# Gate logits from transposed fp16 parts of the rows instead of from rows turned on TensorE

## The chip, the core and the metric

The kernel is one program on one NeuronCore of a Trainium2 chip. The metric is the device time in microseconds. The engines are TensorE (PE, with its weight loads as PEld), VectorE (DVE), ScalarE (ACT), GpSimd (POOL) and the queue engine SyncE (SP), which here only issues transfers. ACT and POOL issue some transfers as well.

## The reference

Input x is 8 x 512 tokens of 256 numbers. First attention, then a mixture of experts, both on normalised rows and both added to what they got:

```python
x = x + attn(layernorm(x), W_qkv, b_qkv, W_out, b_out)   # 16 heads of 16, causal
xn = layernorm(x) * gamma + beta
probs = softmax(xn @ gate_w)                             # 8 experts
w, idx = top_k(probs, 2); w = w / sum(w)
h = gelu(xn @ w1[e] + b1[e]); out_e = h @ w2[e] + b2[e]  # 256 -> 1024 -> 256
x = x + sum over the two chosen e of w[e] * out_e
```

The kernel computes an expert only for the tokens that chose it.

## The kernel before, in words

**Stages.** From 0 to some 122 us the eight batches are normalised and projected to q, k and v. Then come 32 attention units of four heads each, four units to a batch. Behind them stand 39 expert tiles of up to 256 gathered tokens. Between these, the side work of each batch b runs: output projection, residual, second normalisation, the gate, the choice of two experts, the ranks in the experts' lists.

**Order.** Every engine goes through one timetable, written by hand: `at(tick, stage, n)`. A unit has 48 ticks, an expert tile 42; each engine takes its own stages in order of ticks, and waits for semaphores in them. So a wait in a stage holds up everything behind it on that engine. The side work of batch b is placed from a base 192 ticks after that of batch b - 1 (a batch is four units).

**A unit.** `combo` (L660) runs score matmuls on PE (L656 transposed, L628 and L641 for the maxima); ACT takes the exponential (L905, L902), DVE the maxima (L1225 to L1231); `weigh` (L700) multiplies with v. The transposed scores go round three PSUM banks (`TURNS`, banks 4, 5, 6). Side work takes its banks out of the same round (`take_side`), so the next use of a bank waits until the copy named in `TAKEN_BY` has emptied it. `keep_o`, `move_o`, `keep_inverse`, `move_inverse`, `load_unit`, `load_v` and `top_in` are transfers of a unit, issued by SP; `top_in` brings row maxima to the stack that the next unit's scores read.

**The side work that the change touches,** for batch b:

- `out_proj` (L714, L715) projects two halves of the tokens into a bank each; ACT's `copy_out` (L950) moves a half to `turned`; DVE's `add_out` (L1248) adds x, loaded again into `rows`, and writes `x2`.
- After normalisation `rows` holds xn scaled by a power of two; `acc_out` (L1974) stores the residual out of `x2`; then `row_high` on ACT (L940) and `row_low` on DVE (L1491, its instruction at L1067) write two fp16 parts of `rows` into the memory of `x2`, and `rows_out` (L1966) stores them.
- `turn_x` (L722): PE transposes `rows` in fp32, two groups of four 128x128 blocks; ACT's `copy_x` (L922) moves each group to `turned`.
- `gate` (L731): PE multiplies `turned` by `gate_w` in fp32 into a bank; `copy_gate` (L956) copies the 4 x 8 logits of a partition out; DVE's `choose` follows. `count` (L741) multiplies the choices by triangles of ones in bf16.
- `turned` is shared: `copy_out` of the next batch waits for the gate of the batch before.

**Expert stage.** POOL gathers 256 rows (L1703), SP turns them with transposing transfers (`turn_tokens`, L1887, 71 in all, each one chunk of 128 tokens by 512 fp16), PE does 48 matmuls (L775) and 48 (L793) a tile, ACT the gelu (L986), DVE splits it in two parts, POOL scatters (L1727).

Of the kernel before, what the change touches and what calls it, by code (L numbers as in the profile page):

```python
# [14 lines left out]
P = 128  # L15
# [46 lines left out]
def build(nc, t):  # L62
# [54 lines left out]
    with ctx:  # L117
# [17 lines left out]
        tops_dram = dram("tops_of_rows", (P, 5), F32)  # L135
# [8 lines left out]
        keep = Area(arena, 0, 3088 + 2 * TT - D // 2)  # L144
# [10 lines left out]
        gate_w = keep.take(KC * E, k=KC, e=E)  # L155
        minus_half = keep.take(2 * TT, n=2, t=TT)
# [20 lines left out]
        S_TOP, S_SCALE, S_TMP, S_UNDO = stat[:, 0:8], stat[:, 8:12], stat[:, 16:24], stat[:, 24:28]  # L177
        UNDO_1, UNDO_2 = stat[:, 28:29], stat[:, 29:30]
        SCALE_W = [S_SCALE[:, 0:1], S_SCALE[:, 1:2]]
        SCALE_X, SCALE_H = S_SCALE[:, 2:3], S_SCALE[:, 3:4]  # L180
# [23 lines left out]
        turned = a2.take(KC * T, k=KC, t=T)  # L204
# [10 lines left out]
        all_rows_tops = w_raw[1][:, 0:5 * P]  # L215
# [8 lines left out]
        one_more = a2.take(TT)  # L224
        logit = a2.take(TT * E, t=TT, e=E)
# [151 lines left out]
        for b in range(B):  # L377
# [60 lines left out]
        for j in range(-1, TILES):  # L438
# [10 lines left out]
            if j >= 0:  # L449
# [3 lines left out]
                if j + 2 < TILES:  # L453
# [9 lines left out]
        TAKEN_BY = {"top_turn": "top_copy", "out_proj": "copy_out", "turn_x": "copy_x", "gate": "copy_gate",  # L463
                    "count": "copy_count"}
# [99 lines left out]
        def tensor(pe):  # L564
# [153 lines left out]
            def turn_x(b, k):  # L718
                w.wait_ge(sem("beta_added"), b + 1)
                bank = take_side("turn_x", (b, k))  # L720
                for tt in range(TT):
                    m = pe.transpose(bank[:, tt * P:(tt + 1) * P], rows[:, tt, k * P:(k + 1) * P], ident)  # L722
                m.then_inc(sem("side_made"), 1)
# [84 lines left out]
            for stage, n in timetable:  # L808
# [8 lines left out]
                elif stage == "turn_x":  # L817
                    turn_x(*n)
                elif stage == "gate":
                    gate(n)  # L820
                elif stage == "count":
                    count(n)
                elif stage == "hidden":
                    hidden(*n)
                elif stage == "expert_out":
                    expert_out(*n)


        def scalar(act):
# [89 lines left out]
            def copy_x(b, k):  # L919
                w.wait_ge(sem("out_added"), KC * b + k + 1)  # L920
                w.wait_ge(sem("side_made"), side_made("turn_x", (b, k)))
                act.copy(turned[:, k, :], side_bank("turn_x", (b, k))).then_inc(sem("act_freed"), 1)  # L922

# [22 lines left out]
            def copy_out(b, half):  # L946
                w.wait_ge(sem("side_made"), side_made("out_proj", (b, half)))
                if b > 0:
                    w.wait_ge(sem("side_made"), side_made("gate", b - 1))
                act.copy(turned[:, half, :], side_bank("out_proj", (b, half))).then_inc(sem("act_freed"), 1)  # L950

            def copy_gate(b):
                w.wait_ge(sem("side_made"), side_made("gate", b))
                if b > 0:
                    w.wait_ge(sem("chosen"), b)
                act.copy(logit, side_bank("gate", b)[:, 0:TT * E].rearrange("p (t e) -> p t e", t=TT)).then_inc(  # L956
                    sem("act_freed"), 1)
# [56 lines left out]
            for stage, n in timetable:  # L1014
# [12 lines left out]
                elif stage == "copy_x":  # L1027
                    copy_x(*n)
# [32 lines left out]
        def vector(v):  # L1061
# [115 lines left out]
            def find_scales():  # L1177
# [5 lines left out]
                v.tensor_reduce(S_TMP[:, 4:5], b1_sb, AX.XY, ALU.max, apply_absolute_value=True).then_inc(sem("own_tops"), 1)  # L1183

            def find_scales_2():
                w.wait_ge(sem("all_tops"), 16)
                root = math.ceil(math.sqrt(D))
                m = own.mark(v.tensor_reduce(S_TOP[:, 0:5], all_rows_tops.rearrange("p (q c) -> p c q", c=5), AX.X,
# [8 lines left out]
                m = own.mark(both(S_TOP[:, 3:4], S_TOP[:, 3:4], S_TOP[:, 4:5], ALU.add))  # L1197
                w.wait_ge(own.sem, m)
                m = own.mark(v.tensor_scalar(S_TMP[:, 0:4].bitcast(I32), S_TOP[:, 0:4].bitcast(I32), 23, None,
                                             ALU.logical_shift_right))  # L1200
                w.wait_ge(own.sem, m)
                m = own.mark(v.tensor_scalar(S_TMP[:, 0:4].bitcast(I32), S_TMP[:, 0:4].bitcast(I32), 80.0, 200.0,
                                             ALU.max, ALU.min))
                w.wait_ge(own.sem, m)
                own.mark(v.tensor_scalar(S_TMP[:, 4:8].bitcast(I32), S_TMP[:, 0:4].bitcast(I32), -1.0,
                                         float(127 * 2 + 14), ALU.mult, ALU.add))
# [800 lines left out]
```

## Time and profile before

| | us |
|---|---|
| median of 3 runs | 970.67 (967.7 to 975.95) |
| the profiled execution, its own time | 969.97 |
| its span in the trace | 968.1 |
| PE busy, share of the span | 845.3, 87% |
| DVE busy | 703.9, 73% |
| ACT busy | 573.0, 59% |
| POOL busy | 470.0, 49% |
| mean granted TensorE clock | 0.926 of full |

Busy times are of one profiled execution. PE and PEld overlap. A wait is idle time of an engine just before an instruction, with the instruction or transfer whose end released it. SP's rows are issues of transfers: the time given is that of issuing, and the data land later. A batch's side work appears eight times, with b from 0 to 7: for b = 0 to 4 inside the attention units, for b = 5 at their end, for b = 6 and 7 in the expert stage.

### The profile page before, as it was taken

Reading aid. Unit: us, or ns where it says so; the run is one execution under the profiler, and the core shown is the slowest. Engines: PE = TensorE matmul, PEld = TensorE weight load, DVE = VectorE, ACT = ScalarE, POOL = GpSimd, SP = SyncE. Lnnn points to the kernel's source line nnn. Section 1 sums busy time; section 2 is a strip of 40 time slices with the busy share of each in tenths; the row PEclk is TensorE's granted clock in tenths of the full one; section 3 lists DMA queues with packets and bytes.
Section 4 is the critical chain, followed back from the end, with each engine's and each line's share of the span. In section 5 each row is a group of like instructions: output and inputs, shape, how many; then the busy total and the mean of one; then the engine's idle time right before and its main releaser. Section 6 shows DMA issues by size and latency. Waiting matters only on the chain.

```text
span 968.1 us, 21008 instructions
## 1 busy us (share of the span) xinstructions
PE 845.3 (87%) x6760; PEld 555.1 (57%) x6760; DVE 703.9 (73%) x1566; ACT 573.0 (59%) x1048; POOL 470.0 (49%) x575
## 2 busy tenths in 40 slices
PE   4899977877888978797887897989989999999996
PEld 3555422332433424342423695869868888888875
DVE  6677888878689797979895585766756766656664
ACT  2777466657787686868686462545525445445453
POOL 4100032325545747666567556665467554554441
PEclk9999978887998888898987898989999999999998
DMA  9888658745867676566727873444534444444341
GB/s 203 263 271 280 222 164 232 208 111 176 221 198 223 166 194 172 168 195 177 193 69 242 150 136 64 61 83 96 80 51 78 79 79 73 76 76 83 50 74 23
DMA packets 185046, 139.39 MB, mean 144 GB/s; under 512 B 98064, under 2 KB 167568, under 8 KB 184816
## 3 DMA queue, kind: packets, MB, share of 16 engines
q1 hardware_dynamic: 153840, 95.25, 38.5%
q0 software_dynamic: 15776, 18.95, 12.2%
q10 hardware_dynamic: 15328, 23.86, 7.5%
q8 instruction: 61, 1.00, 0.4%
q14 instruction: 41, 0.34, 0.1%
HBM read 83.63 MB, written 44.80 MB: 133 GB/s over the span
## 4 chain that ended last, share of the span: by engine, by line
PE 57%; DVE 16%; DMA 11%; issue 6%; SPq 4%; ACT 4%; another core or an unknown queue 1%; POOLq 0%; ACTq 0%; POOL 0%; DVEq 0%
PE banks L775 18%; PE banks L793 18%; PE banks L597 5%; PE banks L700 3%; DMA arena<-arena 3%; DVE arena L1228 3%; PE banks L714 3%; PE banks L656 3%; DMA weighed_values<-arena 2%; PE banks L587 2%; DVE weights L1390 2%; PE banks L641 2%; DVE arena L1067 2%; PE banks L628 2%; DVE arena L1230 1%
## 5 line engine op out<-in xcount | busy, mean ns | idle before, releaser
L986 ACT ACTIVATE arena<-banks,arena 128x256 f32<-128x256 f32 (+1 forms) x312 | 152.4, 541 | 207.3 <-issue 101.9
L775 PE MATMUL banks<-arena,weights 128*128 128x256 f16 (+1 forms) x1872 | 211.3, 269 | 16.2 <-issue 9.2
L793 PE MATMUL banks<-weights,arena 128*128 x1704 | 198.0, 275 | 5.9 <-DVE arena L1520 3.2
L775 PEld LDWEIGHTS banks<-arena,weights 128*128 x1872 | 176.2, 99 | 45.5 <-issue 20.3
L1727 POOL DMA_INDIRECT out<-arena x71 | 115.7, 1629 | 158.9 <-DVE arena L1531 113.9
L793 PEld LDWEIGHTS banks<-weights,arena 128*128 128x128 f16 x1704 | 165.8, 99 | 31.8 <-issue 9.9
L656 PE MATMUL banks<-arena 64*128 64x128 f16 (+3 forms) x512 | 119.8, 332 | 36.3 <-DMA arena<-arena 13.0
L1518 DVE TENSOR_SCALAR arena<-arena 128x512 f16<-128x512 f32 (+1 forms) x156 | 76.0, 487 | 76.2 <-ACT arena L986 57.1
L628 PE MATMUL banks<-arena 62*128 62x384 f16 (+3 forms) x512 | 94.3, 326 | 32.4 <-DVE arena L1225 11.7
L1520 DVE SCALAR_TENSOR_TENSOR arena<-arena 128x512 f16<-128x512 f32 (+1 forms) x156 | 110.2, 706 | 5.5
L656 PEld LDWEIGHTS banks<-arena 64*128 64x128 f16 x512 | 38.1, 99 | 123.2 <-issue 39.7
L1228 DVE TENSOR_REDUCE arena<-banks 128x2 f32<-128x1024 f32 x64 | 77.9, 1217 | 30.0 <-PE banks L641 29.7
L905 ACT ACTIVATE arena<-banks,arena 128x512 f32<-128x512 f32 x128 | 81.4, 686 | 21.4 <-PE banks L656 20.9
L905 ACT ACTIVATE weights<-banks,arena 128x512 f32<-128x512 f32 x128 | 80.4, 683 | 15.9 <-PE banks L656 15.7
L1703 POOL DMA_INDIRECT arena<-token_rows,arena x71 | 77.3, 1089 | 21.1 <-issue 18.6
L1674 POOL DMA_INDIRECT slot_tokens<-arena x64 | 68.0, 1062 | 26.0 <-issue 16.5
L1688 POOL TENSOR_SCALAR_AFFINE_SELECT weights<-weights 128x512 f32<-128x512 f32 (+1 forms) x80 | 47.7, 613 | 65.5 <-ACT weights L905 57.5
L1230 DVE TENSOR_REDUCE arena<-banks 128x2 f32<-128x768 f32 x64 | 60.8, 950 | 24.1 <-PE banks L641 21.1
L1531 DVE SCALAR_TENSOR_TENSOR arena<-banks,arena 128x256 f32<-128x256 f32 x71 | 31.4, 480 | 60.4 <-PE banks L793 43.1
L1688 POOL TENSOR_SCALAR_AFFINE_SELECT arena<-arena 128x512 f32<-128x512 f32 (+1 forms) x80 | 48.0, 617 | 35.4 <-ACT arena L905 34.0
L641 PE MATMUL banks<-arena 128*128 128x256 bf16 (+1 forms) x320 | 60.7, 275 | 0.0
L700 PE MATMUL banks<-arena 128*32 128x256 f32 (+3 forms) x512 | 58.0, 533 | 2.7 <-ACT arena L917 2.5
(199 smaller groups left out, 1257.1 us busy)
## 6 DMA issues: line engine op xcount, KB each, us to landing
weights<-in_L_ffn_w ACTq DMA_DIRECT2D x16, 1024.0 KB, 7.6
arena<-in_L_ffn_w SPq DMA_DIRECT2D x32, 512.0 KB
qk_parts<-weights SPq DMA_DIRECT2D x64, 128.0 KB
arena<-qk_parts SPq DMA_DIRECT2D x128, 64.0 KB, 3.3
weighed_values<-arena SPq DMA_DIRECT2D x32, 256.0 KB
token_rows<-arena SPq DMA_DIRECT2D x12, 512.0 KB, 4.3
arena<-qk_parts SPq DMA_DIRECT2D x128, 32.0 KB, 3.4
arena<-weighed_values SPq DMA_DIRECT2D x32, 128.0 KB
```

The lines of the kernel that those rows point to most:

```text
L628: pe.matmul(bank[:, to:to + (qt + 1) * P], q_st[u % 4][half, h, qt * P:qt * P + P], k_st[u % 4][half, h, 0:(qt + 1) * P], start=(to == 0), ...
L641: m = pe.matmul(masked, ident_h, mask, start=False, stop=True, skip_group_check=True)
L656: m = pe.matmul(turn_bank(number)[:, to:to + T - kt * P], k_st[u % 4][half, h, kt * P:kt * P + P], q_st[u % 4][half, h, kt * P:T], start=T ...
L700: m = pe.matmul(banks[32 * h:32 * h + 32, O_BANK, kt * P:T], v_and_ones(u, kt, h), p_T[u % 2][:, h, a:a + width], start=(kt == W_ORDER[0]) ...
L775: m = pe.matmul(bank[:, c * TILE:c * TILE + WIDTH[j]], w1[:, k, wp, f:f + P], xp[:, k, 0:WIDTH[j]], start=(i == 0), stop=(i == len(terms) ...
L793: m = pe.matmul(bank[:, c * D:(c + 1) * D], hp[:, f, c * P:(c + 1) * P], w2[:, f // (FC // 2), wp, f % (FC // 2), :], start=(f == 0 and i ...
L905: act.activation(p_T[u % 2][:, PAIR * h + j, PT_AT[kt]:PT_AT[kt] + T], bank, ACT.Exp, scale=EXP_SCALE).then_inc(sem("exped"), 1)
L986: m = act.activation(h_32[r % 2][:, c, 0:WIDTH[j]], banks[:, 1 + c2, c * TILE:c * TILE + WIDTH[j]], ACT.Gelu, bias=b1_now[j % 2][:, 2 * c2 ...
L1228: m = v.tensor_reduce(out[:, :, slot // 2, 3], pair, AX.X, ALU.max, negate=True)
L1520: v.scalar_tensor_tensor(h_low[:, pair, width], h_32[r % 2][:, :, width], SCALE_H, h_high[:, pair, width], ALU.mult, ALU.subtract).then_in ...
L1688: m = g.affine_select(out=area, in_=area, compare_op=ALU.is_ge, fill=0.0, base=0, pattern=pattern, channel_multiplier=-1)
L1727: g.indirect_dma_start(acc_dram[:, :], bass.IndirectOffsetOnAxis(slot_of(j, c), 0), y[j % 2][:, c, :], None, compute_op=ALU.add).then_inc( ...
```

## The change

The gate no longer reads rows turned by PE. `turn_x` and `copy_x` go. SP issues four transposing transfers a batch, `turn_rows`, each for 128 tokens, out of the fp16 parts in `x2` into a new buffer `rows_T` (in the memory of `turned`). The gate weights are split once into two fp16 parts (`gate_parts`), and the gate is 16 fp16 matmuls of 16 columns a batch in place of 8 fp32 ones: the high and low parts of the rows, each times both parts of the weights. `copy_gate` scales back; `choose` first adds the two halves of the logits. `copy_out` writes `x2` in place of `turned`, and `add_out` adds in place. Since the transfers read `x2`, `copy_out` of batch b + 1 waits for `rows_out` and `rows_turned` of batch b.

In the timetable `acc_out`, `row_high`, `row_low` and `rows_out` stand 10 ticks earlier, `gate` and `copy_gate` 28 ticks later; the choices stay where they were for b < 6 and come 24 ticks later for b = 6 and 7. The scales get one more number, for the gate weights.

```diff
-            at(base + 308, "acc_out", b)
-            at(base + 336, "row_high", b)
-            at(base + 344, "row_low", b)
-            at(base + 348, "rows_out", b)
-            for k in range(KC):
-                at(base + 331 + 14 * k, "turn_x", (b, k))
-                at(base + 336 + 14 * k, "copy_x", (b, k))
-            at(base + 372, "gate", b)
-            at(base + 377, "copy_gate", b)
-
-            base += 48 if b < B - 2 else 0
+            at(base + 298, "acc_out", b)
+            at(base + 326, "row_high", b)
+            at(base + 334, "row_low", b)
+            at(base + 338, "rows_out", b)
+            for tt in range(TT):
+                at(base + 342 + 6 * tt, "turn_rows", (b, tt))
+            at(base + 400, "gate", b)
+            at(base + 405, "copy_gate", b)
+
+            base += 48 if b < B - 2 else 24
...
             def gate(b):
-                w.wait_ge(*side_out("turn_x", (b, 1)))
-                w.wait_ge(sem("x_scaled"), 1)
+
+                w.wait_ge(sem("rows_turned"), 16 * TT * (b + 1))
+                w.wait_ge(sem("scales"), 1)
                 bank = take_side("gate", b)
                 for tt in range(TT):
-                    for k in range(KC):
-                        m = pe.matmul(bank[:, tt * E:(tt + 1) * E], turned[:, k, tt * P:(tt + 1) * P], gate_w[:, k, :],
-                                      start=(k == 0), stop=(k == KC - 1))
+                    for i in range(2 * KC):
+                        m = pe.matmul(bank[:, 2 * E * tt:2 * E * (tt + 1)], rows_T[:, i, tt * P:(tt + 1) * P],
+                                      gate_parts[:, i % KC, :, :].rearrange("p s e -> p (s e)"),
+                                      start=(i == 0), stop=(i == 2 * KC - 1))
...
             def copy_out(b, half):
                 w.wait_ge(sem("side_made"), side_made("out_proj", (b, half)))
                 if b > 0:
-                    w.wait_ge(sem("side_made"), side_made("gate", b - 1))
-                act.copy(turned[:, half, :], side_bank("out_proj", (b, half))).then_inc(sem("act_freed"), 1)
+                    w.wait_ge(sem("rows_out"), 16 * b)
+                    w.wait_ge(sem("rows_turned"), 16 * TT * b)
+                else:
+                    w.wait_ge(sem("v_store1"), 16 * (B // 2))
+                act.copy(x2[:, 2 * half:2 * half + 2, :].rearrange("p s d -> p (s d)"), side_bank("out_proj", (b, half))).then_inc(
+                    sem("act_freed"), 1)
...
-                v.tensor_tensor(x2[:, own_x, :], turned[:, half, :].rearrange("p (s d) -> p s d", s=2), rows[:, own_x, :],
-                                ALU.add).then_inc(sem("out_added"), 1)
+                v.tensor_tensor(x2[:, own_x, :], x2[:, own_x, :], rows[:, own_x, :], ALU.add).then_inc(sem("out_added"), 1)
...
+            def turn_rows(b, tt):
+                w.wait_ge(sem("row_low"), b + 1)
+                sp.dma_start(rows_T[:, :, tt * P:(tt + 1) * P], x2[:, tt, :].bitcast(F16), transpose=True).then_inc(
+                    sem("rows_turned"), 16)
+
             def load_again(b):
                 if b > 0:
-                    w.wait_ge(sem("side_made"), side_made("turn_x", (b - 1, 1)))
                     w.wait_ge(sem("row_low"), b)
```

How the order of the queues changes, at two places. First SP, around `rows_out` of batch 2, before (L1815 `load_v`, L1843 `keep_inverse`, L1908 `top_in`, L1966 `rows_out`, L1834 and L1836 `move_o`, L1878 `load_again`, L1970 `shares_out`, L1862 a piece of expert weights):

```order
L1862 DMA arena<-in_L_ffn_w 128x4x256
L1843 DMA inverse_sums<-arena 128x16
L1908 DMA arena<-arena 2x8x128 x2
L1966 DMA token_rows<-arena 128x4x256
L1834 DMA arena<-weighed_values 64x1x512
L1836 DMA arena<-weighed_values 128x1x16
L1878 DMA arena<-in_L_attn_x 128x4x256
L1862 DMA arena<-in_L_ffn_w 128x4x256
L1970 DMA token_rows<-arena 128x4x8
```

And with the change, where L1851 is a piece of weights, L1961 `rows_out`, L1832 `keep_inverse`, L1901 `top_in`, L1823 and L1825 `move_o`, L1871 `load_again`, L1965 `shares_out`:

```order
L1851 DMA arena<-in_L_ffn_w 128x4x256
L1961 DMA token_rows<-arena 128x4x256
L1863 DMA_TRANSPOSE arena<-arena 128x4x128
L1832 DMA inverse_sums<-arena 128x16
L1901 DMA arena<-arena 2x8x128 x2
L1863 DMA_TRANSPOSE arena<-arena 128x4x128
L1823 DMA arena<-weighed_values 64x1x512
L1825 DMA arena<-weighed_values 128x1x16
L1871 DMA arena<-in_L_attn_x 128x4x256
L1863 DMA_TRANSPOSE arena<-arena 128x4x128 x2
L1851 DMA arena<-in_L_ffn_w 128x4x256
L1965 DMA token_rows<-arena 128x4x8
```

`rows_out` moved ahead of `keep_inverse` and `top_in`, and the four transposing transfers stand between `rows_out` and the loads that follow.

Second ACT, around the first half of `copy_out` of batch 3, before, with what each waits for (L917 `copy_o`, L970 the high part of a piece of weights, L950 `copy_out`, L956 `copy_gate`, L905 exponentials, L887 `top_copy`):

```order
L917 COPY arena<-banks 128x512 [waits o_kept,weighed]
L970 ACTIVATE weights<-arena 128x1024 [waits raw_in0]
L950 COPY arena<-banks 128x512 [waits side_made]
L956 COPY arena<-banks 128x32 [waits chosen]
L905 ACTIVATE weights<-banks,arena 128x512 [waits scored_T] x2
L950 COPY arena<-banks 128x512 [waits side_made]
L887 COPY arena<-banks 32x128 [waits top_in,side_made]
```

With the change (L911, L964, L942, L899, L881 in the same parts):

```order
L911 COPY arena<-banks 128x512 [waits o_kept,weighed]
L964 ACTIVATE weights<-arena 128x1024 [waits raw_in0]
L942 COPY arena<-banks 128x512 [waits rows_turned,rows_out,side_made]
L899 ACTIVATE weights<-banks,arena 128x512 [waits scored_T] x2
L942 COPY arena<-banks 128x512 [waits side_made]
L881 COPY arena<-banks 32x128 [waits top_in,side_made]
```

The copy stands in the same place; what it waits for, beside its own bank, is now two transfers of batch 2 in place of batch 2's gate.

## Rows read from the trace of the kernel before

**Rows 1.** Busy time by stretch: us, PE, PEld, DVE, ACT, POOL, PEclk, DMA share, GB/s

```profile
122.00:525.00 403.00, 329.16 (x2650) 139.81 (x2650) 329.78 (x588) 295.78 (x509) 213.44 (x322) 0.86 0.65 180
700.00:800.00 100.00, 94.89 (x845) 82.73 (x844) 64.90 (x181) 42.63 (x89) 60.66 (x61) 0.98 0.44 72
```

**Rows 2.** Waits of the whole span: us in total, times, longest us

```profile
PEld banks L656 <- ACT arena L922: 16.2, 11, 2.3
ACT arena L950 <- PE banks L731: 14.6, 6, 2.8
```

**Rows 3.** Timeline of PE and PEld in batch 2: start us, us, what, idle before

```profile
352.59 0.69 PEld L741 LDWEIGHTS banks<-arena 128*128 128x128 bf16 x14
352.80 0.56 PE L741 MATMUL banks<-arena 128*128 128x8 bf16 x14
357.08 0.60 PE L722 MATMUL banks<-arena 128*128 128x128 f32 x4
368.07 1.85 PE L731 MATMUL banks<-arena 128*128 128x8 f32 x16
371.20 1.54 PE L714 MATMUL banks<-arena 128*128 128x256 f32 x4
```

**Rows 4.** Timeline of DVE in batch 2: the two choices before, and `row_low`

```profile
359.72 0.33 DVE L1067 SCALAR_TENSOR_TENSOR arena<-arena 128x32 f32<-128x32 f32 x2
361.71 1.22 DVE L1067 SCALAR_TENSOR_TENSOR arena<-arena 128x1024 f16<-128x1024 f32 x1
```

**Rows 5.** Timeline of SP in batch 2: start and length of each issue

```profile
359.15 0.43 SPq L1815 DMA_DIRECT2D arena<-v_rows  x1
...
360.30 0.45 SPq L1843 DMA_DIRECT2D inverse_sums<-arena  x1
360.85 1.39 SPq L1908 DMA_DIRECT2D arena<-arena  x2
362.96 0.36 SPq L1966 DMA_DIRECT2D token_rows<-arena  x1
363.51 0.58 SPq L1834 DMA_DIRECT2D arena<-weighed_values  x1
364.13 0.71 SPq L1836 DMA_DIRECT2D arena<-weighed_values  x1
364.89 0.55 SPq L1878 DMA_DIRECT2D arena<-in_L_attn_x  x1
```

**Rows 6.** Transposing transfers by line; landings in the chain of waits; their queue, 910:955

```profile
L1887 SPq DMA_TRANSPOSE arena<-arena x71: 1189/1259/2650, 526.3 to 944.3; - x71
...
299.49 4.64 DMA out<-arena
...
527.71 9.17 DMA arena<-arena
...
921.00 3.39 DMA arena<-arena
...
q1 hardware_dynamic: 3264, 0.79, 9.2%
```

**Rows 7.** Busy time by stretch, around batch 2's `rows_out` and the copy

```profile
360.00:372.00 12.00, 10.96 (x93) 6.93 (x92) 9.37 (x16) 9.33 (x16) 8.78 (x12) 0.98 0.92 240
```

**Rows 8.** Timeline of ACT: before and at batch 3's `copy_out`

```profile
367.10 1.16 ACT L970 ACTIVATE weights<-arena 128x1024 f16<-128x1024 f32 x1
370.01 0.58 ACT L950 COPY arena<-banks 128x512 f32<-128x512 f32 x1 [1.75 <-PE banks L731]
```

**Rows 9.** The same in the first and the last of five batches: SP, DVE, ACT

```profile
256.66 0.45 SPq L1815 DMA_DIRECT2D arena<-v_rows  x1
265.99 0.58 ACT L950 COPY arena<-banks 128x512 f32<-128x512 f32 x1 [2.48 <-PE banks L731]
...
467.61 0.17 DVE L1364 COPY arena<-arena 128x8 f32<-128x8 f32 x1
478.48 0.58 ACT L950 COPY arena<-banks 128x512 f32<-128x512 f32 x1 [2.45 <-PE banks L731]
```

More of the change, by code:

```diff
@@ L141, in build @@
         banks = ctx.enter_context(nc.psum_tensor("banks", [P, 8, 512], F32))
-        keep = Area(arena, 0, 3088 + 2 * TT - D // 2)
+        keep = Area(arena, 0, 3088 + 2 * TT - D // 2 + KC * E)
         ident = keep.take(P)
@@ L155, in build @@
         gate_w = keep.take(KC * E, k=KC, e=E)
+        gate_parts = keep.take(KC * 2 * E // 2, F16, k=KC, s=2, e=E)
         minus_half = keep.take(2 * TT, n=2, t=TT)
@@ L203, in build @@
         sums = [a2.take(HG * TT) for _ in range(2)]
-        turned = a2.take(KC * T, k=KC, t=T)
+        a2.at = -(-a2.at // 8) * 8
+        rows_T = a2.take(2 * KC * T // 2, F16, k=2 * KC, t=T)
         x2 = a2.take(TT * D, t=TT, d=D)
@@ L224, in build @@
         one_more = a2.take(TT)
+        logit_parts = a2.take(TT * 2 * E, t=TT, s=2, e=E)
         logit = a2.take(TT * E, t=TT, e=E)
@@ L462, in build @@
         BANKS_A_UNIT = len(E_USES)
-        TAKEN_BY = {"top_turn": "top_copy", "out_proj": "copy_out", "turn_x": "copy_x", "gate": "copy_gate",
-                    "count": "copy_count"}
+        TAKEN_BY = {"top_turn": "top_copy", "out_proj": "copy_out", "gate": "copy_gate", "count": "copy_count"}
         uses, side, freed = [], {}, {"act_freed": 0, "exped": 0}
@@ L917, in copy_o @@
                 act.copy(o_raw, banks[:, O_BANK, :]).then_inc(sem("o_copied"), 1)
[L919 to L922, printed above, removed]
             def scale_rows(b, tt):
@@ L948, in copy_out @@
                 if b > 0:
[L949 to L950 removed]
+                    w.wait_ge(sem("rows_out"), 16 * b)
[4 more added lines that the diff above has]
+                    sem("act_freed"), 1)
             def copy_gate(b):
                 w.wait_ge(sem("side_made"), side_made("gate", b))
+                w.wait_ge(sem("scales"), 1)
                 if b > 0:
                     w.wait_ge(sem("chosen"), b)
[L956 to L957 removed]
+                act.activation(logit_parts.rearrange("p t s e -> p (t s e)"), side_bank("gate", b)[:, 0:TT * 2 * E],
+                               ACT.Copy, scale=UNDO_GATE).then_inc(sem("act_freed"), 1)
             def copy_count(b):
@@ L1196, in find_scales_2 @@
                 w.wait_ge(own.sem, m)
-                m = own.mark(both(S_TOP[:, 3:4], S_TOP[:, 3:4], S_TOP[:, 4:5], ALU.add))
+                m = own.mark(both(S_TOP[:, 3:4], S_TOP[:, 3:4], S_TOP[:, 5:6], ALU.add))
+                exponent, up = S_TMP[:, 0:5].bitcast(I32), S_TMP[:, 5:10].bitcast(I32)
                 w.wait_ge(own.sem, m)
-                m = own.mark(v.tensor_scalar(S_TMP[:, 0:4].bitcast(I32), S_TOP[:, 0:4].bitcast(I32), 23, None,
-                                             ALU.logical_shift_right))
+                m = own.mark(v.tensor_scalar(exponent, S_TOP[:, 0:5].bitcast(I32), 23, None, ALU.logical_shift_right))
@@ L1216, in find_scales_2 @@
+                w.wait_ge(own.sem, m)
+                v.scalar_tensor_tensor(gate_parts[:, :, 1, :], gate_w, SCALE_GATE, gate_parts[:, :, 0, :], ALU.mult,
+                                       ALU.subtract)
+                v.tensor_tensor(UNDO_GATE, S_UNDO[:, 2:3], S_UNDO[:, 4:5], ALU.mult)
                 v.tensor_tensor(UNDO_1, S_UNDO[:, 0:1], S_UNDO[:, 2:3], ALU.mult)
@@ L1296, in choose @@
                     w.wait_ge(*side_out("gate", b))
-                else:
-                    w.wait_ge(own.sem, choose_at[0])
+                    choose_at[0] = own.mark(both(logit, logit_parts[:, :, 0, :], logit_parts[:, :, 1, :], ALU.add))
+                w.wait_ge(own.sem, choose_at[0])
                 if part == 0:
@@ L1949, in sync @@
                     turn_tokens(n)
+                elif stage == "turn_rows":
+                    turn_rows(*n)
                 elif stage == "table":
```

48 lines of the change are left out of this document (16 added, 32 removed).

## Prediction

> **What bounds the kernel now.** I began with busy time by stretch, and there the kernel splits in two. From 122 to 525 us (attention) PE is busy 329 of 403 us, DVE 330, ACT 296, the DMA engines 0.65; nobody is full, and the units are held up by handing banks back and forth between PE, ACT and DVE. From 700 us on PE is busy 95% and every microsecond taken from it there is a microsecond of the span [rows 1]. So the same PE work has two prices: full price in the expert stage, and in attention only what a wait in the chain makes of it.
>
> Next the waits that the change touches. PE's weight loads waited 16.2 us, 11 times, for `copy_x` (L922), which has to empty a bank of the three before scores can go on. ACT waited 14.6 us, 6 times, before `copy_out` (L950), because `turned` is still read by the gate of the batch before [rows 2]. Both go away.
>
> Then the PE rows of one batch, b = 2: four fp32 transposes 0.60 us, the gate 1.85 us, and 14 bf16 matmuls of `count` with eight columns 0.56 us [rows 3].
>
> **The new wait.** `copy_out(b + 1)` now writes x2, so it waits for `rows_turned` of batch b: all four transposing transfers landed. They are issued by SP at ticks 342 to 360 from the batch's base, the copy stands at 373 from that base. What counts is when SP gets there. Behind the waiting copy on ACT are all exponentials of the next unit; behind it on PE is `out_proj`'s second half, which waits for a bank that this copy frees; DVE waits for both.
>
> I work the time out for b = 2. Start R of `rows_out`: it needs `load_v` issued (359.15 + 0.43) and `row_low`. `row_low` stood behind a maximum at 361.71; the change puts it right behind the two choices that end at 360.05, and it takes 1.22, so R = 361.3 instead of 362.96 [rows 4, 5]. From R, SP issues `rows_out` 0.36, one transposition, `keep_inverse` 0.45, `top_in` 1.39, one transposition, `move_o` 0.58 + 0.71, `load_again` 0.55, one transposition; then the fourth starts. A transposition holds SP 1.26 us (median of 71) [rows 6]. With 0.05 between issues: 0.36 + 0.45 + 1.39 + 1.29 + 0.55 + 3 x 1.26 + 0.45 = 8.27, so the fourth starts at 369.6.
>
> Its landing is not in the trace for this place. The nearest rows: 3.39 us from its issue with a calm queue (at 921.00), 9.17 with the DMA engines full (from 527.71) [rows 6]. From 360 to 372 us the engines are 0.92 busy [rows 7], nearer to the full case, but plain transfers of 512 KB in attention land in 4.64 [rows 6]. I take 4.64 and keep 3.39 and 9.17 as ends.
>
> With 3.39 it lands at 373.0; before, ACT resumed with `copy_out` at 370.01 [rows 8]: +2.9. The same for the others, with 8.7 in place of 8.27 where a `load_raw` (0.4) comes between: b = 0 from `load_v`'s end 257.15: 268.8 against 265.99, +2.8; b = 1 +2.3; b = 3 +0.9; b = 4 from `row_low`, 467.8 + 1.22 = 469.0: 481.1 against 478.48, +2.6 [rows 9]. Sum of the five +11.5; with 4.64 five times 1.25 more: **+17.8**. What `turn_x` and the old gate cost between R and the copy is replaced by this and not taken off again.
>
> Order and resumption: before, the second half of `out_proj` began 1.19 after `copy_out` (371.20 against 370.01 [rows 3, 8]), since gate and scores lay before it; now the scores are done during the wait and it begins when the bank is free, 0.58 after. **-3.0** over five.
>
> **The gate** comes 28 ticks later on PE, 16 matmuls of 16 columns. By `count`, 16/14 of its 0.69 us of weight loads [rows 3] is 0.8 us. In attention five times: **+4.0**. By then the transfers have landed, so it adds no wait of its own.
>
> **Expert stage**, b = 6 and 7: four groups of transposes at 0.60 and two gates 1.85 - 0.8: **-4.5**, full price. Their transposing transfers are issued between those of the tokens; SP mostly waits there, and the gate stands 40 ticks behind them. Choices come 24 ticks (6 us) later for these batches; the first gather that needs them is some 160 ticks off: nothing.
>
> **Boundary**, b = 5: its gate now falls where PE waits for the first tokens anyway (that wait is the 9.17 us row). But four more transfers go through full DMA engines ahead of those tokens. Six transposing transfers took 9.2% of 45 us of all sixteen engines, 0.69 us each [rows 6]; four are 2.8. I take half, **+1.4**.
>
> **The rest.** ACT loses two copies of 0.6 us a batch, within the stretch already replaced. DVE gains one addition of 128x32 a batch, some 0.2 us on an engine 82% busy, and a few instructions once in `find_scales_2`, off the path: 0 to +2, taken as 0. `top_in` moves behind `rows_out` and one transfer (about +1.2 us in issue); at b = 2 it was issued at 360.85, and the scores that need it come after the gate, at 369.92: 9 us of cover, of which a transfer like the calm one uses some 5 with its two issues. It is covered, and again by the longer wait on ACT.
>
> Sum: 17.8 - 3.0 + 4.0 - 4.5 + 1.4 = +15.7. The profiled execution took 969.97 us, 0.7 below the median of 970.67; **969.97 + 15.7 = 986**.
>
> **Two rules of the skill.** The trace shows a transposition of four 128x128 blocks landing in 3.39 us, while PE turns four fp32 blocks in 0.60 [rows 3, 6]. The Trainium skill (VectorE: DVE Perf Modes, The three transpose paths) gives 390 ns for TensorE and 1309 ns for DMA for a 128x128 bf16 block and advises TensorE where PSUM will do: it speaks against this change, and an estimate from it, 4 x 1.31 = 5.2 us in place of 4.64, would make the sum 989. The rows put a transposing transfer of 131 KB at 0.69 us of all engines, 190 GB/s [rows 6]. The Trainium skill (Advanced Engine Details and Errata, X-Bar Transpose (TRN2)) calls such transfers as fast as plain ones, 350 to 400 GB/s; that would halve the boundary term and give 985. The trace shows half that rate.
>
> **Rivals.**
> 1. *SP's queue overflows* (chance 0.12). From 359 to 366 SP issues nearly without a gap [rows 5], and four transpositions are 5 us more per 52 us batch. If what is behind (loads, `keep_o`, `acc_out`) comes 4 us late in each of five batches, or transfers land in 9.17 instead of 4.64, it is +20 more: 1006. Against it: the stalled unit gives SP time to catch up.
> 2. *Wait and gain cancel* (0.26). The first `turn_x` lies before `row_low`. Without it PE is free 0.6 earlier, ACT 0.58, and one bank wait of 16.2 / 11 = 1.5 goes: R up to 2.7 earlier, five times -13.5: 972. For it: these waits are real. Against: in b = 0 and 1 R hangs on SP's own order (`load_v`), which does not move.
> 3. *Faster* (0.17). The last transfer lands before ACT wants the copy, and the new wait does not exist. Then each of five batches wins the wait for the gate 14.6 / 6 = 2.4, two groups of transposes 1.2, half of the bank waits 16.2 / 6 / 2 = 1.35, less the new gate 0.8: -4.1 each, -21; with -4.5 and +1.4 it is -24: 946. It decides at 368.3 in b = 2 (end of the copy's forerunner L970, 367.10 + 1.16 [rows 8]), that is 7 us after R, where the rows give 11.7 at least. For it: SP would have to run well ahead, or ACT arrive later than I think; half such a case gives about 958.
>
> **Numbers.** My forecast has 0.45; its own range is 978 (landing 3.39 and a little of rival 2) to 998. The range takes in rival 2 and half of rival 1, and reaches to the mild form of rival 3: 959 to 1003; outside lie most of rival 3 and part of rival 1, under 0.2. One per cent (9.7 us) is about what a measurement tells from no change. Faster than 961: rival 3, 0.17. Within: rival 2 and the lowest end of mine, 0.27. Slower than 980: the rest, 0.56.
>
> **What would show it.** In the profile after: ACT idle before `copy_out`'s first half in batches 1 to 5, released by a transfer arena<-arena, for some 4 us or more, and PE idle before the second `out_proj`; no wait of PE for a copy of turned rows; the gate at 0.8 us; the expert stage some 4 us shorter; attention ending 15 to 20 us later. It is wrong if that idle time on ACT is under 2 us (rival 3), or if it is there and attention ends no later (rival 2).

## The result, and the profile after

The changed kernel takes **1009.68 us** (median of 4 runs, 1008.93 to 1010.67) against 973.31 (4 runs, 967.7 to 976.18) of the kernel before, run beside it: ratio 1.0366, 95% interval 1.0323 to 1.0409. The forecast was 986, its range ended at 1003. The direction was right, the loss 2.5 times as large as worked out: 39.8 us between the profiled spans (1007.9 less 968.1) against 15.7 forecast. (The medians lie 36.4 us apart.)

First the two stretches of [rows 1] in the changed kernel, with the same columns. In the same 403 us of attention every engine does less, at a lower mean granted clock of TensorE (0.81 for 0.86); 700 to 800 us, where TensorE bounds, is much as before.

```profile
122.00:525.00 403.00, 301.31 (x2396) 123.05 (x2395) 303.18 (x516) 262.72 (x445) 186.06 (x288) 0.81 0.68 175
700.00:800.00 100.00, 96.12 (x882) 84.43 (x880) 67.45 (x185) 46.92 (x95) 60.13 (x59) 0.98 0.49 84
```

The waits of the whole span answer to [rows 2]: us in total, times, longest us. L942 is `copy_out`, L715 `out_proj`, L1238 `add_out`, L1232 the reciprocal of the sums that `move_o` loads.

```profile
ACT arena L942 <- DMA arena<-arena: 65.7, 6, 20.3
DVE arena L1232 <- DMA arena<-weighed_values: 28.3, 12, 14.2
PEld banks L715 <- ACT arena L942: 27.0, 4, 9.0
PE banks L715 <- ACT arena L942: 25.6, 4, 8.7
DVE arena L1238 <- ACT arena L942: 23.7, 5, 10.7
```

The 16.2 us for `copy_x` and the 14.6 for the gate are gone, and 65.7 us stand in their place. TensorE and VectorE stand behind that copy, as the order of the queues said. The second line, VectorE's wait for what `move_o` loads, grew as well; in the kernel before it was:

```profile
DVE arena L1238 <- DMA arena<-weighed_values: 9.1, 3, 4.8
```

ScalarE's timeline answers to [rows 8, 9]: the first half of `copy_out` in batches 1, 3 and 6 (start, length, what, idle before and what ended it). The others of batches 1 to 5 waited 8.66 to 9.97.

```profile
275.17 0.58 ACT L942 COPY arena<-banks 128x512 f32<-128x512 f32 x1 [8.22 <-DMA arena<-arena]
...
392.87 0.58 ACT L942 COPY arena<-banks 128x512 f32<-128x512 f32 x1 [9.05 <-DMA arena<-arena]
...
577.28 0.58 ACT L942 COPY arena<-banks 128x512 f32<-128x512 f32 x1 [20.31 <-DMA arena<-arena]
```

Now TensorE around the second of these copies, to be held against [rows 3]: the second half of `out_proj`, and the new gate.

```profile
393.51 2.07 PE L715 MATMUL banks<-arena 128*128 128x256 f32 x4 [6.15 <-ACT arena L942]
...
400.98 0.56 PE L726 MATMUL banks<-arena 128*128 128x16 f16 x16
```

The half begins 0.64 after the copy as forecast (0.58), and the gate takes 0.56 for 1.85. But the half is slower, 2.07 for 1.54. TensorE had been busy for 1.38 us of the 8 us from 384 on, and during the half its granted clock was 0.50, the lower of its two levels (1.2 GHz). The same stretches by busy time (the columns of [rows 1]), and behind them that of the half in the kernel before, where the mean was 0.62, between the levels:

```profile
384.00:392.00 8.00, 1.38 (x8) 0.41 (x8) 2.92 (x5) 0.00 (x0) 6.94 (x10) 0.64 0.67 136
393.50:395.60 2.10, 2.09 (x6) 1.55 (x7) 0.69 (x1) 1.12 (x2) 0.00 (x0) 0.50 1.05 204
...
371.20:372.80 1.60, 1.60 (x8) 1.14 (x7) 1.40 (x3) 0.65 (x2) 1.16 (x2) 0.62 0.90 137
```

The chain of waits through batch 1's rows tells why the copy comes so late (start, us, what). L1961 is `rows_out`, L1863 a transposing transfer, L1901 `top_in`, L1851 a load of weights; the gaps of under 0.1 us between the issues are left out.

```profile
317.67 0.36 SPq L1961
318.08 2.65 SPq L1863
320.83 0.53 SPq L1832
321.46 0.71 SPq L1901
322.22 0.66 SPq L1901
322.93 1.68 SPq L1851
324.65 1.22 SPq L1863
325.92 0.59 SPq L1823
326.54 0.54 SPq L1825
...
327.46 0.40 SPq L1871
327.92 1.22 SPq L1863
329.20 5.28 DMA arena<-arena
334.57 0.59 ACT arena L942
```

Of the 16.9 us from `rows_out` to the copy 11.5 are SyncE's own time, one issue behind the other, until it reaches the fourth transfer (317.67 to 329.20); only 5.28 lie between the start of that one's issue and its landing. At the boundary, batch 5 with the expert stage behind it, the chain of waits has it in the extreme (L1880 the tokens' transposing transfers, L771 the first expert matmuls):

```profile
556.45 6.99 SPq L1863
563.48 3.73 SPq L1863
...
570.71 3.29 SPq L1880
574.06 4.89 DMA arena<-arena
579.07 1.97 PE banks L771 x9
```

Two single issues held SyncE for 6.99 and 3.73 us. The first begins while ScalarE issues six loads of late weights, 3 MB (from 555.33 to 559.88), and the tokens' own transfers (L1880) queue behind. By the list of issues (count, KB of each, median us from issue to landing) the six loads were long in landing:

```profile
weights<-late_weights ACTq DMA_DIRECT2D x6, 512.0 KB, 15.5
```

Two engines wait for batch 5's rows there. ScalarE stands 20.31 us before the copy, and TensorE 14.45 us before the gate of batch 5, which the change has moved to this place. In the kernel before TensorE's wait at this boundary was 6.42 us, for the first tokens. The gate, the first expert matmuls, and those of the kernel before:

```profile
577.23 0.59 PE L726 MATMUL banks<-arena 128*128 128x16 f16 x16 [14.45 <-DMA arena<-arena]
...
579.07 3.17 PE L771 MATMUL banks<-arena,weights 128*128 128x256 f16 x20 [0.23 <-DMA arena<-arena]
...
537.05 1.25 PE L775 MATMUL banks<-arena,weights 128*128 128x256 f16 x5 [6.42 <-DMA arena<-arena]
```

### The profile page after: what moved, and what is told of

Same layout as the page of the kernel before. It is cut to its first block, busy times and chain, and to the rows that moved or that the text cites. A ratio compares the mean times of both kernels' runs of the same rounds, so it can differ in the third digit from the quotient of the medians.

```text
span 1007.9 us, 20895 instructions
## 1 busy us (share of the span) xinstructions
PE 836.9 (83%) x6696; PEld 542.4 (54%) x6696; DVE 699.3 (69%) x1577; ACT 565.1 (56%) x1032; POOL 462.5 (46%) x575
## 3 DMA queue, kind: packets, MB, share of 16 engines
q1 hardware_dynamic: 171248, 99.52, 40.9%
## 4 chain that ended last, share of the span: by engine, by line
PE 53%; DVE 16%; DMA 11%; SPq 9%; issue 8%; ACT 1%; POOLq 0%; POOL 0%; ACTq 0%; another core or an unknown queue 0%; DVEq 0%
PE banks L771 20%; PE banks L789 18%; PE banks L598 5%; DMA arena<-arena 3%; DVE arena L1222 3%; PE banks L715 3%; SPq L1863 2%; PE banks L701 2%; DMA inverse_sums<-arena 2%; DVE weights L1379 2%; DVE arena L1059 2%; PE banks L588 2%; DVE arena L1224 2%; DMA arena<-weighed_values 2%; DMA weighed_values<-arena 1%
## 5 line engine op out<-in xcount | busy, mean ns | idle before, releaser
L771 PE MATMUL banks<-arena,weights 128*128 128x256 f16 (+1 forms) x1872 | 212.1, 269 | 16.7 <-issue 15.6
L771 PEld LDWEIGHTS banks<-arena,weights 128*128 x1872 | 176.0, 99 | 46.3 <-issue 20.9
L789 PE MATMUL banks<-weights,arena 128*128 x1704 | 195.1, 274 | 0.0
L657 PE MATMUL banks<-arena 64*128 64x128 f16 (+3 forms) x512 | 122.8, 338 | 37.6 <-DMA arena<-arena 18.7
L657 PEld LDWEIGHTS banks<-arena 64*128 64x128 f16 x512 | 38.9, 100 | 124.1 <-issue 41.2
L899 ACT ACTIVATE arena<-banks,arena 128x512 f32<-128x512 f32 x128 | 81.3, 687 | 20.1 <-PE banks L657 19.9
L899 ACT ACTIVATE weights<-banks,arena 128x512 f32<-128x512 f32 x128 | 80.2, 683 | 13.1 <-PE banks L657 12.8
L1692 POOL DMA_INDIRECT arena<-token_rows,arena x71 | 74.9, 1055 | 20.9 <-issue 18.3
L1224 DVE TENSOR_REDUCE arena<-banks 128x2 f32<-128x768 f32 x64 | 60.8, 950 | 23.2 <-PE banks L642 22.9
L1663 POOL DMA_INDIRECT slot_tokens<-arena x64 | 65.7, 1027 | 21.1 <-issue 17.1
L715 PE MATMUL banks<-arena 128*128 128x256 f32 x128 | 45.4, 495 | 34.4 <-ACT arena L942 25.6
```

Of the source, the lines that this page charges most:

```text
L657: m = pe.matmul(turn_bank(number)[:, to:to + T - kt * P], k_st[u % 4][half, h, kt * P:kt * P + P], q_st[u % 4][half, h, kt * P:T], start=T ...
L771: m = pe.matmul(bank[:, c * TILE:c * TILE + WIDTH[j]], w1[:, k, wp, f:f + P], xp[:, k, 0:WIDTH[j]], start=(i == 0), stop=(i == len(terms) ...
L789: m = pe.matmul(bank[:, c * D:(c + 1) * D], hp[:, f, c * P:(c + 1) * P], w2[:, f // (FC // 2), wp, f % (FC // 2), :], start=(f == 0 and i ...
L899: act.activation(p_T[u % 2][:, PAIR * h + j, PT_AT[kt]:PT_AT[kt] + T], bank, ACT.Exp, scale=EXP_SCALE).then_inc(sem("exped"), 1)
L1224: v.tensor_reduce(out[:, :, slot // 2, 2], pair[:, :, 0:3 * P], AX.X, ALU.max, negate=True)
```

## The experiments

Ratios are each kernel's time to the kernel before's on its own chip, with 95% intervals. The first four ran on one chip (before: 954.8 us, 7 runs), the last four on another (before: 956.63, 13 runs). Microseconds between two ratios are taken at 955. The ratios are not the quotients of the medians, and differ from them by up to 0.003 (e5: 1.0428, by the medians 1.0398).

The microseconds in the first four expectations were set on the scale of the first result, where the kernel before took 973.31. On these chips it takes some 18 less, so they have to be read as ratios: for e1 theory A's 950 to 972 is 0.976 to 0.999, theory B's 990 to 1005 is 1.017 to 1.033.

In e1, e2 and e7 the gate does not read the rows; these tell of time alone.

**Theory A**: the stall costs, that is ScalarE's copy waits for transfers that land late, and TensorE and VectorE wait behind it. **Theory B** (rival 1 of the prediction): the transfers' load costs, on SyncE and the DMA engines, whether anyone waits for them or not.

### e1_no_wait: transfers without a wait

```
-sp.dma_start(rows_T[:, :, tt * P:(tt + 1) * P], x2[:, tt, :].bitcast(F16), transpose=True)
+sp.dma_start(rows_T[:, :, tt * P:(tt + 1) * P], arena[:, 0:256].bitcast(F16), transpose=True)
 def copy_out(b, half):
...
-        w.wait_ge(sem("rows_turned"), 16 * TT * b)
```

> The transposing transfers read the first 1 KB of constants of each partition in place of x2, same size, same place in SP's queue, same gate behind them; copy_out therefore waits for rows_out only (the logits and so the choices are meaningless, the number of expert tiles is fixed). Theory A (ACT standing at copy_out for the last transfer is the whole loss): the idle time of ACT before that copy, 65.7 us in six batches, goes, and with turn_x gone as well the time falls to 950 to 972. Theory B (SP's queue and the DMA engines are overfilled by the 32 transfers, whoever waits): the loss stays for the most part, 990 to 1005.

Measured 965.72 us, 1.0105 (1.0047 to 1.0162), between the marks of the two theories. The copy's wait is then 0.026, 25 us, of the 35 (1.0366 less 1.0105; the two ratios were taken apart), and 10 us of loss are left that this wait does not explain. The gate still waits for the transfers here. TensorE stood idle for them before it, in the units of the list of waits:

```profile
PE banks L726 <- DMA arena<-arena: 14.3, 4, 9.8
```

The 9.8 are at batch 5's gate, the rest at three gates inside attention. So e1 takes away the copy's wait and not every wait for the transfers.

### e2_no_turns: neither transfers nor wait

```
-for tt in range(TT):
+for tt in range(TT if b == 0 else 0):
     at(base + 342 + 6 * tt, "turn_rows", (b, tt))
...
-w.wait_ge(sem("rows_turned"), 16 * TT * (b + 1))
+w.wait_ge(sem("rows_turned"), 16 * TT)
```

The last two lines are in `gate`; the edit of e1 is in it as well.

> As e1_no_wait, and the transposing transfers of batches 1 to 7 are left out as well (the gate reads what batch 0's left). Theory A: 28 transfers less of load alone, 0 to 8 us under e1_no_wait. Theory B: this one comes back to 965 or lower while e1_no_wait does not, a gap of 20 us or more between the two.

Measured 944.69 us, 0.9889 (0.9839 to 0.9939). So taking TensorE's transposes, their copies and the fp32 gate away is worth 1.1%, and 28 transfers cost 21 us (965.72 less 944.69, same chip) though no copy waits for them; the waits of the gate are in the 21. Both theories hold in part, A with some 25 us and B with some 21. The two traces lie 29.4 us apart, one execution each: 11.8 of them between the copies of batches 0 and 5, 4.6 from there to the first expert matmul, and 13.3 in the expert stage.

### e3_turns_first and e4_turns_after_top: the same transfers elsewhere in SyncE's queue

```
-at(base + 342 + 6 * tt, "turn_rows", (b, tt))
+at(base + 338, "turn_rows", (b, tt))
```

for e3, right behind `rows_out`, and for e4, behind `keep_inverse` and `top_in`:

```
-at(base + 342 + 6 * tt, "turn_rows", (b, tt))
+at(base + 345, "turn_rows", (b, tt))
```

> The changed kernel with all four transposing transfers right behind rows_out (tick 338 in place of 342 to 360). Theory A: the last lands some 4 us sooner after rows_out in batches 0 to 4, and in batch 5 it is issued before the late weights' loads fill the rings, which gives back 12 us or more: 970 to 985 in all. top_in is issued 4 us later, and PE may wait for it a little. Theory B: no change, since the same transfers go through the same queue: 1005 to 1012.

> The changed kernel with all four transposing transfers at tick 345: behind keep_inverse and top_in, ahead of move_o and load_again. Theory A: the last lands some 2 to 3 us sooner than in the changed kernel in batches 0 to 4, and part of batch 5's wait goes: 978 to 995, between the changed kernel and e3_turns_first unless top_in was what e3_turns_first lost. Theory B: no change, 1005 to 1012.

e3 measured 977.85 us, 1.0261 (1.0203 to 1.0319), e4 971.15, 1.0177 (1.0127 to 1.0228). Both beat the changed kernel, against theory B's "no change". As ratios theory A's ranges were 0.997 to 1.012 for e3, which missed it, and 1.005 to 1.022 for e4, which met it. In e3 ScalarE's wait for rows is down to 17.0 us in three places, but TensorE waits for what `top_in` loads; in e4 the wait is 32.3. SyncE in e4, batch 2 (start and length of each issue; L1863 the four, L1823 `move_o`):

```profile
366.95 0.36 SPq L1961 DMA_DIRECT2D token_rows<-arena  x1
367.40 2.06 SPq L1832 DMA_DIRECT2D inverse_sums<-arena  x1
369.56 1.41 SPq L1901 DMA_DIRECT2D arena<-arena  x2
371.02 6.10 SPq L1863 DMA_TRANSPOSE arena<-arena  x4
377.17 0.58 SPq L1823 DMA_DIRECT2D arena<-weighed_values  x1
```

Four in a row hold SyncE 6.10 us here (5.16 to 6.10 in batches 0 to 5); spread among plain transfers, the four of the changed kernel's batch 2 take 3.14 + 2.85 + 2.52 = 8.51. The last one starts sooner and nothing stands between. The waits of e3, for comparison (L657 the scores that need `top_in`):

```profile
PE banks L657 <- DMA arena<-arena: 31.3, 16, 4.3
ACT arena L942 <- DMA arena<-arena: 17.0, 3, 11.9
```

TensorE's 31.3 are 22.8 in e4. What e3 gains on ScalarE over e4 it gives back there: the wait moved.

The 11.9 of e3 and 13.75 us of e4's 32.3 stand before batch 6's copy. In both all four transfers of batch 5 were issued in a row, in 5.55 and 5.90 us, with no issue above 1.7. Still the last one landed about 12.5 and 14.2 us after its issue began, where in batches 0 to 4 of the changed kernel that takes 4.3 to 5.4. So long issues are not all of the boundary: in these two versions it is the landing.

### e5_after_again: the changed kernel as a yardstick

> The changed kernel itself, on the chip of the three runs beside it, as their yardstick. If the ratio to the kernel before is a property of the kernels, it is 1.037 again (1.032 to 1.041).

Measured 994.71 us, 1.0428 (1.0345 to 1.0512), just above the range I gave. The interval overlaps the first (1.0323 to 1.0409); ScalarE's wait is 67.1 us in 6, and from batch 0's copy to batch 6's it is 361.9 us for 361.7. What makes this trace shorter (995.5 us for 1007.9) is mostly the expert stage, 414.6 us for 428.8 with the same kernel.

### e6_apart: the projection copied to two idle buffers

```
 def copy_out(b, half):
     w.wait_ge(sem("side_made"), side_made("out_proj", (b, half)))
-    if b > 0:
-        w.wait_ge(sem("rows_out"), 16 * b)
-        w.wait_ge(sem("rows_turned"), 16 * TT * b)
...
-    act.copy(x2[:, 2 * half:2 * half + 2, :].rearrange("p s d -> p (s d)"), side_bank("out_proj", (b, half))).then_inc(
-        sem("act_freed"), 1)
+    act.copy((o_dense, o_inverse)[half][1], side_bank("out_proj", (b, half))).then_inc(sem("act_freed"), 1)
 def add_out(b, half):
...
+    if b > 0:
+        w.wait_ge(sem("rows_out"), 16 * b)
+        w.wait_ge(sem("rows_turned"), 16 * TT * b)
...
-    v.tensor_tensor(x2[:, own_x, :], x2[:, own_x, :], rows[:, own_x, :], ALU.add).then_inc(sem("out_added"), 1)
+    made = (o_dense, o_inverse)[half][1].rearrange("p (s d) -> p s d", s=2)
+    v.tensor_tensor(x2[:, own_x, :], made, rows[:, own_x, :], ALU.add).then_inc(sem("out_added"), 1)
 def move_o(u):
...
+        if k == 1:
+            w.wait_ge(sem("out_added"), KC * (b - 1) + 1)
 def move_inverse(u):
...
+        if k == 1:
+            w.wait_ge(sem("out_added"), KC * (b - 1) + 2)
```

> The changed kernel, but the copies of the projection's two halves no longer go over x2: the first goes to o_dense[1], the second to o_inverse[1], which both lie idle between the division of this batch and the loads of the next one's third unit. Only the addition on VectorE writes x2, and so it alone waits for the transposing transfers. Theory A (the stall of ScalarE is what costs, some 24 us of the 36): the ratio to before falls from 1.037 to about 1.012, what the run without the wait gave (1.0105), and ScalarE's 65.7 us of idle time ahead of the copies go. Rival (the wait only moves, to VectorE's addition, and VectorE's queue then holds up ScalarE and TensorE alike): 1.030 or more, with VectorE idle 8 us ahead of each first addition.

Measured 972.44 us, 1.0192 (1.0126 to 1.0258): 22 us less than e5 beside it. That difference (0.024) is the one expected (0.025), so the rival is out. The ratio itself is 7 us above the mark of 1.012, which lies just outside the interval; the changed kernel itself came out 6 us higher on this chip. ScalarE and VectorE in batch 2's part:

```profile
379.43 0.57 ACT L937 COPY arena<-banks 128x512 f32<-128x512 f32 x1
```

```profile
389.00 0.69 DVE L1238 TENSOR_TENSOR arena<-arena 128x512 f32<-128x512 f32 x1 [2.45 <-DMA arena<-arena]
```

The copy waits for no transfer. VectorE now waits for the rows, 2.45 us here and 23.0 in six places over the span, 10.4 the longest, where ScalarE had waited 67.1 in the kernel beside it. The boundary keeps most of its wait: TensorE stands 12.73 us before batch 5's gate (14.09 in e5).

### e7_plain: the same bytes without transposing

```
-sp.dma_start(rows_T[:, :, tt * P:(tt + 1) * P], arena[:, 0:256].bitcast(F16), transpose=True)
+sp.dma_start(rows_T[:, :, tt * P:(tt + 1) * P], arena[:, 0:256].bitcast(F16).rearrange("p (k t) -> p k t", k=2 * KC))
```

The minus line is that of e1_no_wait.

> The run without the wait (the transfers read constants in place of x2, the gate's values are meaningless), with the 32 transposing transfers replaced by plain copies of the same bytes, 131 KB each, into the same buffer. In that run the transfers' presence cost some 21 us (1.0105 with them, 0.9889 without). If it is their transposing (long issue on SyncE, many small packets), the ratio falls to 0.990 to 0.995, with an issue of about 0.5 us each. If it is the bytes and the places in a full queue that any transfer takes, it stays at 1.005 to 1.012.

Measured 952.16 us (10 runs), 0.9981 (0.9942 to 1.0019), between the two marks I set, nearer to the first. Against e1's 1.0105 the transposing itself costs about 12 us, against e2's 0.9889 the bytes and their places in the queue about 9. Another chip's yardstick stands between these ratios, by the intervals each difference is good to 6 or 7 us, and by the medians they are 15 and 6. The 12 hold a wait of the gate too: TensorE's wait for the transfers before it is 14.3 us in e1 and 7.6 here, all of it at batch 5's gate. One line by source for the transfers of this run and one of e1's, count, then ns min/median/max:

```profile
L1862 SPq DMA_DIRECT2D arena<-arena x32: 594/659/1797, 259.8 to 649.5; - x32
```

```profile
L1862 SPq DMA_TRANSPOSE arena<-arena x32: 1201/1586/7541, 264.0 to 676.4; - x32
```

The packets are not it: 171248 on that queue in e1, 170736 with plain copies.

### e8_one_transfer: one issue in place of four

```
-for tt in range(TT):
-    at(base + 342 + 6 * tt, "turn_rows", (b, tt))
+at(base + 342, "turn_rows", (b, 0))
...
-sp.dma_start(rows_T[:, :, tt * P:(tt + 1) * P], x2[:, tt, :].bitcast(F16), transpose=True)
+sp.dma_start(rows_T, x2.rearrange("p t d -> p (t d)").bitcast(F16), transpose=True)
```

The addresses in `gate` and the counts of `rows_turned` change to match.

> The changed kernel with one transposing transfer a batch of 512 KB (16 blocks of 128x128) at the place of the first, in place of four of 131 KB. The bytes and the wait stay. If the number of issues on SyncE, and what stands between them, is what makes the last one land late: the copy waits 4 to 5 us less in each of batches 1 to 5, ratio 1.015 to 1.025. If the rate of the transposing itself limits: the landing takes 4 x as long from one issue, the issue blocks SyncE for 5 us or more, and top_in behind it comes later: 1.035 to 1.045.

Measured 971.65 us, 1.0175 (1.0106 to 1.0243), 23 us less than e5: the first branch. SyncE, then ScalarE, in batch 2's part:

```profile
373.63 0.36 SPq L1960 DMA_DIRECT2D token_rows<-arena  x1
374.04 6.25 SPq L1862 DMA_TRANSPOSE arena<-arena  x1
380.39 0.52 SPq L1831 DMA_DIRECT2D inverse_sums<-arena  x1
```

```profile
384.00 0.58 ACT L941 COPY arena<-banks 128x512 f32<-128x512 f32 x1 [2.81 <-DMA arena<-arena]
```

The one issue takes 6.25 us, no less than e4's four in a row (6.10); what it saves is all that stood between. The transfer has landed at 384.0, 3.7 us after its issue ended and 10.4 after `rows_out` began; in the changed kernel the copy came 15.9 us after `rows_out` (376.98 to 392.87). In batches 1 to 5 the copies wait 7.3 us in all for the rows, in three places, where e5's wait 47.2 in five: some 8 us less in each, where I expected 4 to 5. The boundary is left as it was: a wait of 19.14 before batch 6's copy.

**Not measured.** No version here whose gate reads the rows beats the kernel before. The two repairs of e6 and e8 touch different things (who waits, and when the last transfer starts); what they give together was not measured, nor with e4's place in the queue, nor was either kernel measured with the late weights loaded at another time. The ceiling is e2's 1.1%, and by e7 even plain transfers cost most of it (9 us, 6 by the medians).

## Why the prediction failed on the size

Copy to copy, from the first halves' starts (batch 0 to 6: before 212.22, 265.99, 316.29, 370.01, 426.32, 478.48, 525.89; after 215.54, 275.17, 334.57, 392.87, 453.08, 513.69, 577.28) the 39.8 us of span fall into four terms, from one execution of each kernel:

| term | forecast | measured |
|---|---|---|
| ahead of the first copy | 0 | +3.3 |
| batches 1 to 5 (17.8 - 3.0 + 4.0) | +18.8 | +31.9 |
| boundary: copy 5 to copy 6 +16.2, then to the first expert matmul 1.8 us for 11.2 | +1.4 | +6.8 |
| expert stage (428.8 for 431.05 us) | -4.5 | -2.2 |

The first row was in no term of mine, and its cause stays open: the first copy came at 214.1 to 219.0 us in the nine traces of the changed kernel and its versions, at 212.22 in the one of the kernel before.

1. **The mechanism was right.** ScalarE waits for transfers arena<-arena in batches 1 to 5, above 4 us each, TensorE waits before the second `out_proj`, nobody waits for turned rows, attention ends later. Rival 3 is out, since in the changed kernel a wait of 8 us or more stood in every batch; rival 2 is out, since attention ended later all the same (batch 6's copy by 51.4 us).
2. **The step that failed: "A transposition holds SP 1.26 us (median of 71)".** The 71 of [rows 6] were issued in the expert stage, where the DMA engines are less busy (0.44 for 0.65 [rows 1]). Among attention's plain transfers one took 1.2 to 3.14. In batch 2 the fourth started 11.6 us after R (376.98 to 388.59) in place of 8.27. Over the five batches the way from R to the copy took 77.6 us for the 65.8 of the prediction (8.27 or, three times, 8.7, and 4.64 each), that is 11.8 of the 13.1 by which the row of batches 1 to 5 is over. Of the 11.8, the issues of the three transposing transfers ahead of the fourth are 8.5 (27.4 us for 18.9), the plain issues between them 2.0, the landing 1.2. The row had the sign in its own maximum, 2650, and I used the median at a place whose engines I had just read as 0.92 busy [rows 7]. I put the crowding into the landing and not into the issue. That crowding is what stretches an issue is my reading; no run set it apart.
3. **The landing was right in attention.** Batch 2: 388.6 to 392.87, 4.3 us against 4.64; batch 1: 5.28; the five together 24.4 for 23.2. At the boundary it was not, as point 5 says. In attention the far ends (3.39, 9.17) were not needed.
4. **"The rest", taken as 0.** e1 against e2 prices the 28 transfers at 21 us without the copy's wait, part of it waits of the gate. Rival 1 had the mechanism of late loads, with 0.12, "if what is behind comes 4 us late in each of five batches". It should have been a term, since every microsecond of SyncE's issue lay ahead of loads that others wait for. `top_in` was called covered by 9 us; the changed kernel has TensorE idle 2.53 us for it in batch 2 and 18.7 us in 11 places over the span. But this wait is not the price of the transfers alone. The kernel before has 13.0 us of it, and e2, without 28 of the transfers, 24.2:

```profile
PE banks L656 <- DMA arena<-arena: 13.0, 10, 3.4
...
PE banks L657 <- DMA arena<-arena: 24.2, 15, 3.9
```

The clock was no term either: the first four matmuls of the second half took 10.4 us in the five batches together (2.07 in each) and 7.1 in the kernel before. These 3.3 us lie on the way from a copy to the next R, which all the same came out within 1.2 us of the forecast (220.6 us for 219.4).

5. **The boundary** was worked out as the engines' time for the bytes (2.8 us, halved), with the gate free because it "falls where PE waits for the first tokens anyway". In fact the gate was the wait: TensorE's 14.45 us for batch 5's rows took the place of the 6.42 for the first tokens. Issues of 6.99 and 3.73 us were part of it, and the landing the other: 13.8 us from the start of the last issue (563.48) to the copy, and about as long in e3 and e4, whose issues were short. In e7 a plain issue at this place took 0.65 and 0.82 us, and TensorE still waited 7.58 us for the data. The late weights' loads themselves took 15.5 us to land, and an estimate from their 3 MB and the 240 GB/s of [rows 7] is 13 us. That they are what holds the rows up fits all this and is not shown, as no run moved them.
6. **The gate**: 0.56 us for the 0.8 taken from `count`, a small error on the safe side.
7. **The expert stage** gained half of what was worked out, but -2.2 us says little, since the same kernel took 14.2 us less there in e5. Among the traces of the eight experiments the stage took 414.6 to 418.0 us in the six versions with all transposing transfers, 408.1 with plain copies (e7) and 404.7 with none for these batches (e2). So the transfers of batches 6 and 7 probably cost more than the 4.5 us that the transposes and the old gate had; these are single executions, and no run took that pair alone.

By the ratios the change is, at 955 us: 11 gained for work taken off TensorE and ScalarE (e2), 9 lost for the bytes, 12 for their being transposed (e7, e1), and 25 for the copy over x2 (the first result against e1; 22 by e5 against e6, which keeps a wait on VectorE, 31 by e5 against e1). The terms are good to some 6 us each.

With the rows turned by transfers the kernel takes 1.0366 and 1.0428 of the time that it takes with TensorE's transposes. By the Trainium skill (VectorE: DVE Perf Modes, The three transpose paths, and the table of its Rules for kernel authors) TensorE is the cheaper place for such a block where PSUM will do; the runs agree. Its per-block price leaves out the issue, which in this case held SyncE's later loads back as well.

In e7 and e1 the issue of the same 131 KB took 659 ns plain and 1586 transposing (medians), and the kernel times differ by about 12 us. By the Trainium skill (Advanced Engine Details and Errata, X-Bar Transpose (TRN2)) such transfers go as fast as plain ones. The measurement speaks against it for the issue and for the time of the kernel; how fast the bytes themselves move was not compared.

## What to carry to other kernels

A transfer has a price on the queue that issues it, ahead of any wait for it: read the issue's length at the place where it will stand, with the engines as busy as there, not from a calm stage, and charge it to every load behind it. When a result is copied over a buffer that transfers still read, look first for a buffer that is idle in just that interval, and let the latest possible step (here the addition) carry the wait. A transfer's landing has to be asked for in every place where something waits for it, the last one too: here one of six places, beside 3 MB of other loads, took about three times as long as the rest. And several small transfers spread through a busy queue land later than one large one: where the last counts, issue them together.

## What was not expected of the hardware

- One issue of a transposing transfer of 131 KB held SyncE from 1.2 to 6.99 us in the changed kernel; plain issues stretched as well in such places (`keep_inverse` 2.06 us in e4, against 0.45 in [rows 5]).
- In attention, issue time went with the bytes more than with the number: 512 KB as one transfer 3.44 to 6.25 us, as four in a row 5.16 to 6.10 (e8, e4, batches 0 to 5).
- With the same bytes and nearly the same packets, transposing cost about 12 us of kernel time over plain copies, with the gate as the only consumer that waited for either.
- Issued early and in a row, the four transfers of batch 5 still landed 12.5 and 14.2 us after the last issue began (e3, e4), with six loads of 512 KB under way, and 4.3 to 5.4 us in batches 0 to 4 of the changed kernel.
